# Top-64 attention: chunk tops stored rank by rank, selection behind its own chunks, ScalarE and TensorE in a new order, loops peeled

## Chip, cores and metric

One core of one Trainium2 chip (trn2) runs the whole program. The metric is the device time of one execution in microseconds; lower is better.

## The reference

The input is x, 2 images of 256 channels and 48x48 = 2304 positions. Two transformer-like layers follow each other. The first has top-k attention:

```python
q, k, v = heads(conv1x1(x, Wq, bq)), heads(conv1x1(x, Wk, bk)), heads(conv1x1(x, Wv, bv))
scores = einsum('bhnd,bhmd->bhnm', q, k) * 32 ** -0.5      # 8 heads of 32, N = 2304
kth = top_k(scores, 64)[0][..., -1:]
masked = where(scores >= kth, scores, finfo.min)
o = einsum('bhnm,bhmd->bhnd', softmax(masked), v)
o = conv1x1(o, Wo, bo) + x
h1 = relu(batchnorm(conv1x1(o, W1, b1)))
x = batchnorm(conv1x1(h1, W2, b2)) + o
```

The second normalises x over the channels, does full softmax attention of the same size, projects it and adds x. Everything is float32. The change touches only the first attention.

## The kernel before

The program is a sequence of stages, each a block in which every engine runs its own list of instructions and waits on semaphores: `project_heads`, `attention_top`, `project_out`, `mlp`, `project_heads`, `attention_full`, `output`. `attention_top` works on tiles of 128 queries against all 2304 keys. Two tiles make a pair; a head has 18 pairs (2 images x 9), and 8 heads make 144 pairs. What happens to a tile:

- TensorE computes the 128x2304 scores into `ps_s` (`score`, L363), ScalarE copies them to `scores_all` (`keep_scores`, L446), which has room for four tiles.
- VectorE takes the eight largest of each of 64 chunks of 36 scores (`chunk_tops`, MAX8, L557, into `top8`). `prepare` takes the eight largest of all that ranks 4 to 8 hold (L565, L567) and the largest of the ranks 1 and 8 (`extremes`, L568).
- ScalarE guesses a threshold from the chunk tops: a scaled sum of ranks 1 and 2 (`guess_place`, L477), then a count of candidates over it by Sign (L480, `balance`).
- VectorE's `select` corrects the guess (L582, L585), counts the candidates above it (L589), masks them (L594), computes `place` (L596), takes the best 24 of the rest in three rounds of MAX8 and MATCH_REPLACE8 (L601, L605), picks the one that is the 64th largest (L609) and flags rows where this can't be sure (`doubt`, L613).
- TensorE counts the flags (`count_doubts`, L390, L392), ScalarE copies the counts (`keep_any`, L467), and VectorE loads them into a register and branches (`hand_on`): where there is a doubt it counts the whole row again (L631) and, if need be, finds the threshold by eight full rounds (L644). Then it writes `steep_kth` (L666) and `minus_max` (L667).
- ScalarE writes a steep Relu penalty (L462), GpSimd subtracts it from the scores (L539), ScalarE takes the exponential with its sum (L450).
- TensorE transposes the 18 blocks of the tile in groups of four (`turn`, L373, two PSUM buffers `ps_t`), ScalarE copies each group (`keep_turned`, L457), TensorE weighs the values (`weigh`, L382). At the end of a pair ScalarE copies `parts` (L522), TensorE adds the quadrants (L401), ScalarE writes `o_all` (`finish`, L486).

The order within an engine is written out by hand. VectorE is a pair or more ahead: while it takes the chunk tops of pair p it selects pair p-1 behind the eighth chunk and hands it on behind the twentieth. ScalarE, in the step of pair p, makes the second guess of pair p+1 behind a copy of scores and the first guess of pair p+2 at the end. ScalarE and TensorE run `Fori(0, HEADS)` with 18 unrolled steps, and VectorE peels the first two pairs and the last head and runs `Fori(0, HEADS - 1)`. Past the last pair, ScalarE and TensorE still do the scores, guesses and penalties that their loop bodies hold.

Of the kernel before, what the change touches and what calls it, by code (L numbers as in the profile page):

```python
# [47 lines left out]
ROUNDS = TOPK // 8  # L48

# [223 lines left out]
def attention_top(nc, cst, operands, q_parts, k_parts, v_all, o_all, sums):  # L273
# [5 lines left out]
    with ctx:  # L279
# [13 lines left out]
        weighted, compared = sb("weighted", [P, 2, CHUNKS, 2]), sb("compared", [P, 2, CHUNKS, KEEP])  # L293
        minus_first, balance = sb("minus_first", [P, 2]), sb("balance", [P, 2])
        factor, guess = sb("factor", [P, 2]), sb("guess", [P, 2])
        above_guess, place = sb("above_guess", [P, 2]), sb("place", [P, 2])
        places, picked = sb("places", [P, WINDOW]), sb("picked", [P, 2, WINDOW])
        extremes, beyond = sb("extremes", [P, 2, 2]), sb("beyond", [P, 2])
# [22 lines left out]
        HEAD_PAIRS = B * PAIRS  # L321
        block = ctx.enter_context(nc.Block())
# [24 lines left out]
        def _(pe):  # L347
            pe.sem_inc(parts_ready, 1)
            pe.sem_inc(o_kept, 1)

            def score(s, h, tile, first=False):

                ahead, s = divmod(s, HEAD_TILES)
                b, pair = s // MCH, s // 2
                if s % 2 == 0:
                    pe.wait_ge(q_loaded[pair % AHEAD_Q],
                               (h + ahead) * (32 * HEAD_PAIRS // AHEAD_Q) + 32 * (pair // AHEAD_Q + 1))
                if s % MCH == 0:
                    pe.wait_ge(k_loaded[b], (h + ahead) * 64 + 64)
                if not first:  # L360
                    pe.wait_ge(scores_kept, tile)
                for c, n in SCOLS:
                    last = pe.matmul(ps_s[:, c:c + n], q_ring[pair % AHEAD_Q][:, P * (s % 2):P * (s % 2) + P],  # L363
                                     k_stack[b][:, c:c + n], start=True, stop=True)
                last.then_inc(scores_done, 1)

            def turn(s, g, tile):

                if s % 2 == 1 or g >= 2:
                    pe.wait_ge(turned_kept, tile * NTG + g - 1)  # L370
                m0, n = TGROUPS[g]
                for m in range(n):
                    last = pe.transpose(ps_t[(NTG * s + g) % 2][:, P * m:P * m + P],  # L373
                                        probs[s % 2][:, P * (m0 + m):P * (m0 + m) + P], cst["ident"][:, :])
                last.then_inc(turned, 1)

            def weigh(s, g, tile):
# [1071 lines left out]
```

## Time and profile before

| | |
|---|---|
| median of 3 runs | 5313.2 us (5310.25 to 5314.53) |
| profiled execution | 5306.61 us, span 5304.8 us |
| mean granted clock of TensorE | 0.825 |
| PE busy | 4161.1 us, 78% |
| DVE (VectorE) busy | 4384.5 us, 83% |
| ACT (ScalarE) busy | 4144.0 us, 78% |
| POOL (GpSimd) busy | 1502.1 us, 28% |

In the profile L-numbers are lines of the kernel. "Idle before" is the time an engine stood idle just ahead of an instruction or group, and behind the arrow stands what ended it; "issue" is a wait that the profile doesn't explain by a semaphore. On VectorE and ScalarE the next instruction may start a little before the last one has ended, so the distance of two starts is what an instruction costs its engine, and its duration is what someone who waits for its result sees.

### The profile page before, as it was taken

What the parts mean: (1) busy time and instruction counts of PE and PEld (TensorE: products, weight loads), DVE (VectorE), ACT (ScalarE), POOL (GpSimd) and SP (SyncE); (2) the same over time, 40 slices, a digit from 0 to 9 for tenths busy, and PEclk for the clock granted to TensorE, in tenths of its full rate; (3) what the DMA queues carried; (4) which work ended last, traced back from release to release, by engine and by line L of the source; (5) the groups of instructions that cost most, each with busy time, mean ns of one, the idle gap of its engine ahead of it and who ended that gap; (6) DMA issues with size and microseconds to landing.
All of it is one profiled execution on the core that took longest, in us unless ns stands there. A gap on an engine that the chain in (4) does not pass through costs nothing. (4 is left out here: it accounts for less than half of the span.)

```text
span 5304.8 us, 112543 instructions
## 1 busy us (share of the span) xinstructions
PE 4161.1 (78%) x32161; PEld 2808.6 (53%) x32161; DVE 4384.5 (83%) x25258; ACT 4144.0 (78%) x6082; POOL 1502.1 (28%) x362
## 2 busy tenths in 40 slices
PE   8576477776777557767777667798999999999997
PEld 4344345444444334444454445443567777777774
DVE  4899999998999899999999999430378888888885
ACT  2798599988998678988999889544268888888884
POOL 0354354444454334444454445100100000000000
PEclk9677677777777777777777777899799999999999
DMA  5000000000000000000000000100320101111012
GB/s 208 6 17 16 5 16 8 18 16 7 18 17 16 7 15 8 17 16 8 17 17 9 17 16 8 56 8 6 143 77 25 34 24 33 33 25 34 24 33 89
DMA packets 79566, 154.52 MB, mean 29 GB/s; under 512 B 8120, under 2 KB 49464, under 8 KB 73528
## 3 DMA queue, kind: packets, MB, share of 16 engines
q1 hardware_dynamic: 78904, 146.72, 9.8%
q8 instruction: 290, 4.75, 0.4%
q14 instruction: 372, 3.05, 0.2%
HBM read 99.50 MB, written 47.19 MB: 28 GB/s over the span
## 5 line engine op out<-in xcount | busy, mean ns | idle before, releaser
L539 POOL TENSOR_TENSOR a_probs<-a_scores,a_probs 128x2304 f32<-128x2304 f32 x288 | 1460.1, 5092 | 1778.5 <-ACT a_probs L462 1778.5
L557 DVE MAX8 a_top<-a_scores 128x8 f32<-128x36 f32 x18432 | 1830.8, 179 | 46.8 <-ACT a_scores L446 46.1
L373 PE MATMUL a_ps_t<-ident,a_probs 128*128 128x128 f32 x5184 | 973.7, 325 | 704.0 <-ACT a_probs_t L457 570.1
L373 PEld LDWEIGHTS a_ps_t<-ident,a_probs 128*128 128x128 f32 x5184 | 672.6, 164 | 992.2 <-ACT a_probs_t L457 708.6
L462 ACT ACTIVATE a_probs<-a_scores,a_steep_kth 128x2304 f32<-128x2304 f32 x290 | 641.2, 2211 | 295.0 <-DVE a_minus_max L667 295.0
L1117 PE MATMUL b_ps_t<-ident,b_soft 128*128 128x128 f32 x5184 | 744.1, 279 | 20.9 <-issue 19.3
L1242 DVE TENSOR_SCALAR_CACHE_REDUCE b_soft<-b_ps_s 128x2304 f32<-128x2304 f32 x288 | 735.2, 2553 | 26.9 <-PE b_ps_s L1101 9.0
L457 ACT ACTIVATE a_probs_t<-a_ps_t 128x512 f32<-128x512 f32 (+1 forms) x1440 | 727.2, 545 | 20.4 <-PE a_ps_t L373 7.4
L1117 PEld LDWEIGHTS b_ps_t<-ident,b_soft 128*128 128x128 f32 x5184 | 581.0, 141 | 204.0 <-issue 80.4
L1199 ACT ACTIVATE b_soft<-b_soft,b_minus_max 128x2304 f32<-128x2304 f32 x288 | 638.1, 2216 | 43.6 <-issue 26.0
L450 ACT ACTIVATE a_probs<-a_probs,a_minus_max 128x2304 f32<-128x2304 f32 x288 | 638.0, 2215 | 28.6 <-issue 18.5
L363 PE MATMUL a_ps_s<-a_k_stack,a_q_ring 128*128 128x512 f32 (+1 forms) x1465 | 647.5, 601 | 14.7 <-ACT a_scores L446 9.8
L446 ACT ACTIVATE a_scores<-a_ps_s 128x2304 f32<-128x2304 f32 x292 | 607.0, 2079 | 12.3 <-PE a_ps_s L363 12.3
L382 PE MATMUL a_ps_o<-a_probs_t,a_v 128*32 128x128 f32 x10368 | 579.0, 303 | 0.2
L1206 ACT ACTIVATE b_soft_t<-b_ps_t 128x512 f32<-128x512 f32 (+1 forms) x864 | 419.4, 520 | 174.6 <-PE b_ps_t L1117 174.3
L363 PEld LDWEIGHTS a_ps_s<-a_k_stack,a_q_ring 128*128 128x128 f32 x1465 | 433.2, 319 | 156.6 <-ACT a_scores L446 64.5
L1101 PE MATMUL b_ps_s<-b_k_stack,b_q_ring 128*128 128x512 f32 (+1 forms) x1440 | 451.0, 411 | 8.4 <-DVE b_soft L1242 5.0
L1248 DVE COPY b_soft_t<-b_ps_t 128x512 f32<-128x512 f32 x576 | 385.1, 687 | 83.1 <-PE b_ps_t L1117 82.7
L382 PEld LDWEIGHTS a_ps_o<-a_probs_t,a_v 128*32 128x32 f32 x10368 | 263.0, 115 | 226.0 <-issue 113.7
L1078 POOL COPY b_v<-v_all 128x576 f32 x16 | 10.6, 667 | 1293.1 <-PE b_ps_o L1136 1185.8
L1136 PE MATMUL b_ps_o<-b_soft_t,b_v 128*32 128x256 f32 x5184 | 368.5, 384 | 0.6 <-issue 0.6
L401 PE MATMUL a_ps_o<-add_up,a_parts 128*128 128x32 f32 x576 | 148.6, 397 | 259.1 <-ACT a_parts L522 259.1
(128 smaller groups left out, 4216.7 us busy)
## 6 DMA issues: line engine op xcount, KB each, us to landing
a_k_stack<-k_parts SPq DMA_DIRECT2D x72, 288.0 KB, 6.0
b_k_stack<-k_parts SPq DMA_DIRECT2D x72, 288.0 KB, 6.1
a_q_ring<-q_parts SPq DMA_DIRECT2D x294, 64.0 KB
b_q_ring<-q_parts SPq DMA_DIRECT2D x294, 64.0 KB
k_parts<-p_high SPq DMA_DIRECT2D x36, 256.0 KB, 2.1
k_parts<-p_rest SPq DMA_DIRECT2D x36, 256.0 KB, 2.2
q_parts<-p_high SPq DMA_DIRECT2D x36, 256.0 KB, 2.0
q_parts<-p_rest SPq DMA_DIRECT2D x36, 256.0 KB, 2.0
```

What stands on the lines that cost most here:

```text
L363: last = pe.matmul(ps_s[:, c:c + n], q_ring[pair % AHEAD_Q][:, P * (s % 2):P * (s % 2) + P], k_stack[b][:, c:c + n], start=True, stop=True)
L373: last = pe.transpose(ps_t[(NTG * s + g) % 2][:, P * m:P * m + P], probs[s % 2][:, P * (m0 + m):P * (m0 + m) + P], cst["ident"][:, :])
L382: last = pe.matmul(ps_o[rows, P * (s % 2):P * (s % 2) + P], v_s[s // MCH][:, m, :], probs_t[:, m, :], start=m < 4, stop=m + 4 >= MCH)
L446: act.activation(scores_all[:, s % 4, :], ps_s[:, 0:N], ACT.Copy).then_inc(scores_kept, 1)
L450: act.activation(probs[s % 2][:, :], probs[s % 2][:, :], ACT.Exp, scale=SCALE, bias=minus_max[parity][:, s % 2:s % 2 + 1], accum_out=sums[ ...
L457: act.activation(probs_t[:, m0:m0 + n, :], ps_t[(NTG * s + g) % 2][:, 0:n * P].rearrange("p (m q) -> p m q", q=P), ACT.Copy).then_inc(turn ...
L462: act.activation(probs[u][:, :], scores_all[:, 2 * parity + u, :], ACT.Relu, scale=-STEEP, bias=steep_kth[parity][:, u:u + 1]).then_inc(pe ...
L539: pool.tensor_tensor(probs[u][:, :], scores_all[:, 2 * (p % 2) + u, :], probs[u][:, :], ALU.subtract).then_inc(masked_ready, 1)
L557: last = dve.max(top8[s // 2 % 2][:, s % 2, c, :], scores_all[:, s % 4, CHUNK * c:CHUNK * c + CHUNK])
L1117: last = pe.transpose(ps_t[(NTG * s + g) % 2][:, P * m:P * m + P], soft[s % 3][:, P * (m0 + m):P * (m0 + m) + P], cst["ident"][:, :])
L1199: act.activation(soft[s % 3][:, :], soft[s % 3][:, :], ACT.Exp, scale=-1.0, bias=minus_max[s % 3][:, 0:1], accum_out=sums[:, s, cols(h + a ...
L1242: dve.tensor_scalar(soft[s % 3][:, :], ps_s[:, 0:N], -SCALE, None, ALU.mult, ALU.min, accum_out=minus_max[s % 3][:, 0:1]).then_inc(shifted ...
```

## The change

- `top8` is laid out rank by rank: eight places for the rest, then 64 values of rank 1, 64 of rank 2, and so on. MAX8 of a chunk writes its eight results 64 elements apart. The candidates are then one run of 8 + 3x64 = 200 elements (216 before, 16 of them fill). `extremes` come from MAX8 over 64 elements, two for each tile, in place of one reduction. `place` is gone, since `counts` holds 63 - n.
- VectorE selects a pair directly behind its own chunks, between `sort_rest` and the next pair, and hands it on behind the eighth chunk of the next pair. The wait for ScalarE's `balance` now stands behind the pair's own chunks.
- ScalarE makes both guesses of pair p+1 in the step of pair p: the first behind the exponential, the second behind two copies of transposes. The copies of scores move behind the first tile's last transpose copy and in between the second tile's last two; `finish` moves into the next step.
- TensorE has both score tiles of pair p+2 in the step of pair p, one behind the first tile's last `turn`, one behind the second tile's fourth.
- ScalarE and TensorE start two steps early with the parts that exist, loop over seven heads from pair 2 on, and peel the last; what would lie past the last pair is left out.

```diff
-        top8 = [sb(f"top8{n}", [P, 2, CHUNKS + REST, 8]) for n in range(2)]
-        below = sb("below", [P, 2, (CHUNKS + REST) * KEEP])
+        top8 = [sb(f"top8{n}", [P, 2, REST + 8 * CHUNKS]) for n in range(2)]
+        below = sb("below", [P, 2, CANDIDATES])
...
-                    last = dve.max(top8[s // 2 % 2][:, s % 2, c, :], scores_all[:, s % 4, CHUNK * c:CHUNK * c + CHUNK])
+                    last = dve.max(top8[s // 2 % 2][:, s % 2, REST + c:REST + c + 7 * CHUNKS + 1:CHUNKS], scores_all[:, s % 4, CHUNK * c:CHUNK * c + CHUNK])
...
+            rank = lambda tops, u, r, n=1: tops[:, u, REST + r * CHUNKS:REST + (r + n) * CHUNKS]
+            def sort_rest(pair, tops):
+                for u in range(2):
+                    wait_alone(dve, tops_taken, 2 * pair + u + 1)
+                    counted(dve.max(tops[:, u, 0:REST], rank(tops, u, KEEP, 7 - KEEP)))
+            def find_extremes(u, tops):
+                for n, r in enumerate((0, 7)):
+                    counted(dve.max(extremes[:, u, n, :], rank(tops, u, r)))
+            def correct_guess(pair):
                 after(at["n"])
                 dve.wait_ge(balance_ready, 2 * pair + 2)
-                factors = counted(dve.tensor_scalar(factor[:, :], balance[:, :], -STEP / 2,
-                                                    -(1.0 + STEP * (CHUNKS * KEEP / 2 - AIM)), ALU.mult, ALU.add))
+                return counted(dve.tensor_scalar(factor[:, :], balance[:, :], -STEP / 2,
+                                                 -(1.0 + STEP * (CHUNKS * KEEP / 2 - AIM)), ALU.mult, ALU.add))
...
-                counted(dve.tensor_scalar(place[:, :], above_guess[:, :], -1.0, TOPK - 1.0, ALU.mult, ALU.add))
...
             def pair_step(pair, tile, p, before=True):
+                tops = top8[p % 2]
                 def between(c):
                     if c == 7 and before:
-                        select(pair - 1, top8[(p - 1) % 2])
-                    if c == 19 and before:
                         hand_on(pair - 1, (p - 1) % 2)
                 chunk_tops(tile, 2 * p, between)
                 chunk_tops(tile + 1, 2 * p + 1)
-                prepare(pair, top8[p % 2])
+                sort_rest(pair, tops)
+                find_extremes(0, tops)
+                factors = correct_guess(pair)
+                find_extremes(1, tops)
+                select(tops, guess_of(factors))
```

ScalarE's step, before and after (`here`, `before`, `after` and `second` say whether the pair p, p-1, p+1 or p+2 exists; these tests are left out here):

```diff
-                    exponentials(s, h, tile, parity)
-                    keep_scores(s + 4, tile + 4)
-                    guess_place(1, pair + 1, 1 - parity)
-                    keep_turned(s, 0, tile)
-                    keep_turned(s, 1, tile)
-                    exponentials(s + 1, h, tile + 1, parity)
-                    keep_turned(s, 2, tile)
-                    keep_turned(s, 3, tile)
-                    keep_turned(s, 4, tile)
-                    keep_scores(s + 5, tile + 5)
-                    keep_any(pair + 1)
-                    keep_turned(s + 1, 0, tile + 1)
-                    keep_turned(s + 1, 1, tile + 1)
-                    act.wait_ge(kth_ready, pair + 2)
-                    penalty(0, 1 - parity)
-                    keep_turned(s + 1, 2, tile + 1)
-                    keep_turned(s + 1, 3, tile + 1)
-                    keep_turned(s + 1, 4, tile + 1)
-                    penalty(1, 1 - parity)
-                    act.wait_ge(weighed, tile + MCH + 3)
-                    act.activation(parts[:, :], ps_o[:, 0:PAIR], ACT.Copy).then_inc(parts_ready, 1)
-                    guess_place(0, pair + 2, parity)
-                    finish(s, h, pair)
+                exponentials(p, 0, h)
+                guess_place(p + 1, 0, h)
+                keep_turned(p, 0, 0, h)
+                finish(p - 1, h)
+                keep_turned(p, 0, 1, h)
+                guess_place(p + 1, 1, h)
+                keep_turned(p, 0, 2, h)
+                exponentials(p, 1, h)
+                keep_turned(p, 0, 3, h)
+                keep_turned(p, 0, 4, h)
+                keep_scores(p + 2, 0, h)
+                keep_turned(p, 1, 0, h)
+                keep_any(pair + 1)
+                keep_turned(p, 1, 1, h)
+                keep_turned(p, 1, 2, h)
+                penalty(p + 1, 0, h)
+                keep_turned(p, 1, 3, h)
+                keep_scores(p + 2, 1, h)
+                keep_turned(p, 1, 4, h)
+                penalty(p + 1, 1, h)
+                keep_parts(pair)
...
-            with act.Fori(0, HEADS) as h:
-                for p in range(HEAD_PAIRS):
+            for p in range(-2, 2):
+                pair_step(p, 0)
+            with act.Fori(0, HEADS - 1) as h:
+                for p in range(2, HEAD_PAIRS + 2):
+                    pair_step(p, h)
+            for p in range(2, HEAD_PAIRS):
+                pair_step(p, HEADS - 1)
+            finish(HEAD_PAIRS - 1, HEADS - 1)
```

TensorE's step after the change, in the same short form:

```
turn(p,0) groups 0 1 2 | weigh(p,0) 0 | turn 3 | weigh 1 | turn 4 | score(p+2,0)
turn(p,1) group 0 | weigh(p,0) 2 3 4 | turn(p,1) 1 | count_doubts(p+1) | turn(p,1) 2 3
score(p+2,1) | wait any_ready | weigh(p,1) 0 | turn(p,1) 4 | weigh(p,1) 1 2 3 4 | add_quadrants(p)
```

## Rows read from the trace of the kernel before

**Rows 1.** Page, costliest groups: count, busy us, mean ns, idle before

```profile
L450 ACT ACTIVATE a_probs<-a_probs,a_minus_max 128x2304 f32<-128x2304 f32 x288 | 638.0, 2215 | 28.6 <-issue 18.5
```

**Rows 2.** Timeline of VectorE over one ordinary pair: start us, duration us, instruction

```profile
944.99 0.88 DVE L557 MAX8 a_top<-a_scores 128x8 f32<-128x36 f32 x8 [0.18 <-ACT a_scores L446]
945.83 0.17 DVE L582 TENSOR_SCALAR a_factor<-a_balance 128x2 f32<-128x2 f32 x1
...
947.79 0.17 DVE L596 TENSOR_SCALAR a_place<-a_above_guess 128x2 f32<-128x2 f32 x1
...
951.42 0.16 DVE L613 SCALAR_TENSOR_TENSOR a_doubt<-a_beyond,a_kth 128x2 f32<-128x2 f32 x1
...
953.29 0.17 DVE L666 TENSOR_SCALAR a_steep_kth<-a_kth 128x2 f32<-128x2 f32 x1 [0.53 <-issue]
...
953.43 10.58 DVE L557 MAX8 a_top<-a_scores 128x8 f32<-128x36 f32 x108
963.93 0.48 DVE L565 MAX8 a_top<-a_top 128x8 f32<-128x320 f32 x1
...
964.72 0.61 DVE L568 TENSOR_REDUCE a_extremes<-a_top 128x4 f32<-128x256 f32 x1
965.50 0.88 DVE L557 MAX8 a_top<-a_scores 128x8 f32<-128x36 f32 x8 [0.17 <-ACT a_scores L446]
```

**Rows 3.** Timeline of ScalarE over the same pair

```profile
952.15 0.14 ACT L467 ACTIVATE a_any_doubt<-a_ps_o 1x3 f32<-1x3 f32 x1
...
953.56 2.22 ACT L462 ACTIVATE a_probs<-a_scores,a_steep_kth 128x2304 f32<-128x2304 f32 x1 [0.29 <-DVE a_minus_max L667]
...
960.36 0.23 ACT L486 ACTIVATE o_top<-a_ps_o 128x64 f32 x1
961.07 2.21 ACT L450 ACTIVATE a_probs<-a_probs,a_minus_max 128x2304 f32<-128x2304 f32 x1 [0.48 <-POOL a_probs L539]
...
963.28 2.07 ACT L446 ACTIVATE a_scores<-a_ps_s 128x2304 f32<-128x2304 f32 x1
965.25 0.30 ACT L477 ACTIVATE a_weighted<-a_top 128x128 f32<-128x128 f32 x1
...
966.04 0.19 ACT L480 ACTIVATION_READ_ACCUMULATOR a_compared<-a_top,a_minus_first 128x1 f32 x1
966.14 1.06 ACT L457 ACTIVATE a_probs_t<-a_ps_t 128x512 f32<-128x512 f32 x2
```

**Rows 4.** Timeline of GpSimd over the same pair

```profile
955.85 10.14 POOL L539 TENSOR_TENSOR a_probs<-a_scores,a_probs 128x2304 f32<-128x2304 f32 x2 [10.36 <-ACT a_probs L462]
```

**Rows 5.** Timeline of TensorE over the same pair

```profile
951.69 0.24 PE L392 MATMUL a_ps_o<-a_doubt,ones 128*1 128x1 f32 x4
951.86 0.65 PE L373 MATMUL a_ps_t<-ident,a_probs 128*128 128x128 f32 x4
...
963.43 1.97 PE L373 MATMUL a_ps_t<-ident,a_probs 128*128 128x128 f32 x8 [1.66 <-ACT a_probs L450]
```

**Rows 6.** The same timeline, cut after the first four transposes

```profile
963.43 1.12 PE L373 MATMUL a_ps_t<-ident,a_probs 128*128 128x128 f32 x4 [1.66 <-ACT a_probs L450]
```

**Rows 7.** Busy time in stretches: length, busy us, then PEclk 0.50, DMA

```profile
961.10:963.50 2.40, 0.74 (x4) 0.23 (x3) 2.40 (x26) 2.40 (x3) 2.40 (x1) 0.50 0.00 0
```

**Rows 8.** Groups of VectorE by form, 300 to 3300 us

```profile
L589 DVE TENSOR_SCALAR_CACHE_REDUCE a_below<-a_top,a_guess 128x216 f32<-128x216 f32 x267 | 106.3, 436 | 4.8
...
L631 DVE TENSOR_SCALAR_CACHE_REDUCE a_scratch<-a_scores,a_bound 128x2304 f32 x16 | 41.8, 2612 | 3.4 <-issue 3.4
```

**Rows 9.** Timeline of VectorE at a turn of the head loops

```profile
988.32 0.88 DVE L557 MAX8 a_top<-a_scores 128x8 f32<-128x36 f32 x8 [2.51 <-ACT a_scores L446]
```

**Rows 10.** Timeline at the start and the end of the stage

```profile
139.29 0.17 DVE L666 TENSOR_SCALAR a_steep_kth<-a_kth 128x2 f32<-128x2 f32 x1 [1.02 <-issue]
...
3348.28 0.17 DVE L666 TENSOR_SCALAR a_steep_kth<-a_kth 128x2 f32<-128x2 f32 x1 [1.70 <-ACT a_any_doubt L467]
...
3378.15 1.95 DVE L779 RECIPROCAL r_one_by_sum<-sums_top 128x288 f32<-128x288 f32 x1 [29.63 <-PEq L279]
```

More of the change, by code:

```diff
@@ L321, in attention_top, with exists @@
         HEAD_PAIRS = B * PAIRS
+        def exists(pair):
+            return not isinstance(pair, int) or 0 <= pair < ALL_PAIRS
         block = ctx.enter_context(nc.Block())
@@ L403, in add_quadrants, with pair_step @@
                 last.then_inc(added, 1)
-            score(0, 0, 0, first=True)
-            for s in range(1, 5):
-                score(s, 0, s)
-            count_doubts(0)
-            with pe.Fori(0, HEADS) as h:
-                for p in range(HEAD_PAIRS):
-                    pair, tile = h * HEAD_PAIRS + p, h * HEAD_TILES + 2 * p
-                    s = 2 * p
-                    pe.wait_ge(probs_ready, tile + 1)
-                    turn(s, 0, tile)
-                    turn(s, 1, tile)
-                    score(s + 5, h, tile + 5)
+            def pair_step(p, h):
+                pair = h * HEAD_PAIRS + p
+                here, after, second = exists(pair), exists(pair + 1), exists(pair + 2)
+                if here:
+                    for g in range(3):
+                        turn(p, 0, g, h)
@@ L429, in _ @@
-                    weigh(s, 4, tile)
-                    count_doubts(pair + 1)
-                    turn(s + 1, 1, tile + 1)
-                    turn(s + 1, 2, tile + 1)
-                    weigh(s + 1, 0, tile + 1)
-                    turn(s + 1, 3, tile + 1)
-                    weigh(s + 1, 1, tile + 1)
-                    turn(s + 1, 4, tile + 1)
-                    for g in range(2, NTG):
-                        weigh(s + 1, g, tile + 1)
-                    add_quadrants(pair)
-                    score(s + 6, h, tile + 6)
+                    if exists(pair - 1):
+                        pe.wait_ge(o_kept, pair)
@@ new lines, in pair_step @@
+                    weigh(p, 0, 0, h)
+                    turn(p, 0, 3, h)
+                    weigh(p, 0, 1, h)
+                    turn(p, 0, 4, h)
+                if second:
+                    score(p + 2, 0, h)
+                if here:
+                    turn(p, 1, 0, h)
+                    for g in range(2, NTG):
+                        weigh(p, 0, g, h)
+                    turn(p, 1, 1, h)
+                if after:
+                    count_doubts(pair + 1)
+                if here:
+                    turn(p, 1, 2, h)
+                    turn(p, 1, 3, h)
@@ new lines, in pair_step @@
+                if second:
+                    score(p + 2, 1, h)
+                if after:
+                    pe.wait_ge(any_ready, pair + 2)
+                if here:
+                    weigh(p, 1, 0, h)
+                    turn(p, 1, 4, h)
+                    for g in range(1, NTG):
+                        weigh(p, 1, g, h)
+                    pe.wait_ge(parts_ready, pair + 1)
+                    add_quadrants(pair)
+            for p in range(-2, 2):
+                pair_step(p, 0)
@@ L526, in _ @@
+            for p in range(-2, 2):
+                pair_step(p, 0)
+            with act.Fori(0, HEADS - 1) as h:
+                for p in range(2, HEAD_PAIRS + 2):
+                    pair_step(p, h)
+            for p in range(2, HEAD_PAIRS):
+                pair_step(p, HEADS - 1)
+            finish(HEAD_PAIRS - 1, HEADS - 1)
         @block.gpsimd
```

178 lines of the change are left out of this document (86 added, 92 removed).

## The prediction

> **What bounds the kernel now.** I read the page first for where the time lies. The stage that the change touches is the first attention, top-k included; it runs from about 113 to 3378 us [rows 10], some 62% of the span, and everything else is left alone. In it VectorE and ScalarE are both above nine tenths busy, so the shares don't say which of them sets the time. The timelines of one ordinary pair do: the eight chunk maxima that open a pair start at 944.99, the next ones at 965.50 [rows 2]. That is 20.51 us a pair, and it is one closed chain through all four engines:
>
> - eight chunks, then the guess's factor: 944.99 to 945.83, 0.84 [rows 2]
> - factor, guess and the whole selection to `doubt`: 945.83 to 951.42, 5.59 [rows 2]
> - doubt to `steep_kth`: 951.42 to 953.29, 1.87, of which ScalarE's copy of the doubt count starts 0.73 after the doubt, and the load, test and branch that follow take 1.14 [rows 2, 3]
> - to ScalarE's penalty 0.27, to GpSimd's subtraction 2.29 (955.85), from there to the exponential 5.22 (961.07) [rows 2 to 4]
> - exponential to the copy of the scores 2.21, that copy 2.07, and 0.15 until VectorE starts [rows 2, 3].
>
> The sum is 20.51. Every link is tight: VectorE's only idle time outside the branch ends with ScalarE's copy of the scores (0.17 at 965.50) [rows 2]. VectorE's own work is a second bound close below. From the first threshold at 139.29 to the last at 3348.28 there are 143 pairs in 3209 us [rows 10]: 143 x 20.5 = 2932, and the rest is recounts of doubtful rows (16 in the window of [rows 8], some with further rounds), a slower branch now and then, and seven turns of the head loop at some 2.6 us each ("issue" 18.5 us) [rows 1]. The change touches neither how often rows are doubtful nor what a recount costs.
>
> **VectorE's own work.** 120 of 128 chunk maxima are as before: 108 took 10.50 from 953.43 to 963.93, 0.097 apart [rows 2]; I expect no change from writing the eight results 64 elements apart. The selection reads 200 candidates in place of 216. A count over 216 elements lasts 0.436, the same instruction over 2304 2.612 [rows 8]: 1.04 ns an element, so 14 instructions (two counts, two masks, six maxima, four replacements) x 16 elements x 1.04 ns = 0.23 saved. `place` goes: 0.07 (947.79, next at about 947.86). The stretch from the first count to the doubt was 5.59 less 0.40 for factor and guess = 5.19, and becomes 4.88. The extremes' reduction starts at 964.72 and lasts 0.61 [rows 2], which keeps VectorE about 0.50; four maxima over 64 elements take its place, each, between 0.097 for 36 and 0.395 for 320 (963.93 to 964.72, two of them), 0.13, so 0.51: no gain. The factor now waits for the result of the maximum before it (0.24 in place of 0.13), and two maxima fill the gap between factor and guess, so from factor to first count 0.07 + 0.25 + 0.20 = 0.53. The whole: 0.14 + 120 x 0.097 + 0.79 + 0.37 + 0.53 + 4.88 + 0.60 + 1.14 = 20.1 us. Were VectorE the bound, that would be 0.4 less a pair.
>
> **Where the guess now stands.** Before, ScalarE's second guess stood behind the very copy of scores that VectorE's chunks waited for, and ended (966.23) while VectorE took eight chunks. Now VectorE selects a pair right behind its own chunks and must wait for ScalarE's second guess of that pair, which stands in ScalarE's queue behind the exponential of the pair before, the first guess, two copies of transposes and the finish. The closed chain is then, from the exponential's start:
>
> - Exponential: TensorE's transposes start 2.36 later (961.07 to 963.43) [rows 3, 5]. Four of them take 1.12 and eight 1.97 [rows 5, 6], and the first copy can't start before 3.51, the second before 4.36. ScalarE has come to 3.10 with exponential 2.21 and guess 0.89 (965.25 to 966.14), so it waits 0.41; a copy's 0.48 (an estimate, from two in 1.06) and finish 0.25 (0.23 at 960.36) bring it to 4.24, where it waits again 0.12. The second copy ends its turn at 4.84. VectorE's chunks for the second guess are done at 12.0 after `steep_kth` (0.14 + 56 and 64 chunks + 0.2); the guess starts at 0.27 + 7.51 + 4.84 = 12.6, so ScalarE, not VectorE, is late.
> - Guess to its count (966.04 + 0.19) 0.98 [rows 3], VectorE's start 0.12 as before (966.23 to 965.50 + 0.84).
> - Factor to doubt 0.53 + 4.88 = 5.41.
> - Doubt to the copy of the count: 0.73 before, where ScalarE was in a long copy; at least 0.54, since TensorE's counts end 0.51 after the doubt's start (951.69 + 0.24) [rows 5]. I take 0.60. Then 1.14 to `steep_kth`.
> - Penalty, subtraction, exponential: 0.27 + 7.51.
>
> Sum: 4.84 + 0.98 + 0.12 + 5.41 + 0.60 + 1.14 + 7.78 = 20.87, against 20.51: 0.36 longer. Over 143 pairs 51 us. The eight chunks in place of twelve before the branch are no matter: they end 0.9 after the doubt, while the branch ends at 1.74. ScalarE's own work is 20.51 less its idle 0.29 and 0.48 [rows 3], 19.7 us a pair, so it is no bound by busy time, and keeping the scores' copy off the path gains nothing more, since the path that went through it (20.51 less selection's saving) is replaced by this one.
>
> The bounds of that period: the copy of the count may start at 0.54 or, when TensorE is still in a transpose at the low clock ahead of `count_doubts`, at 0.8; the third copy of the odd tile stands between it and the penalty and may push it 0.2. So 20.8 to 21.1, 41 to 84 us.
>
> **Loops, start and end.** A turn of ScalarE's loop left it idle 2.6 us, and VectorE's turn fell inside VectorE's wait for that (2.51 at 988.32) [rows 1, 9]. There are now six turns of all three loops. VectorE's now lies between `doubt` and the branch, on the chain, uncovered. Priced as ScalarE's: 2.6 each, 0 if it hides after all, 3 at most. Six of ScalarE's, 0.2 of each hidden by the earlier end of its step, and six of VectorE's: 14 + 16 = 30 in place of 18, so +12 (-4 to +14).
> Start: the first threshold, at 139.29 [rows 10], came behind eight chunks of the next pair and a second guess; now the selection follows its own chunks at once, is 0.3 shorter, and the branch comes sooner. By the same working 1.1, 0.3 and 0.6, so -2. End: from the last `steep_kth` (3348.28) to the next stage's first VectorE instruction (3378.15) 29.9 us [rows 10], with a pair's scores, guesses and penalties that nobody uses. Without these the last step's chain is 7.8 to the exponential, then 14.3 through both tiles' copies to the finish, 0.5 to leave: 22.6, so -7.
>
> Sum: 51 + 12 - 2 - 7 = +54. The profiled execution took 5306.6 us, 1.8 of it beside its span, and the change would make it 5360.6; the median of the runs is 6.6 higher: **5367 us**.
>
> **Strides and turns against the Trainium skill.** A reading of ranks 3 of 8 apart costs no more per element here than one in a row: the count over 216 strided candidates takes 0.436 and the same instruction over 2304 in a row 2.612, 1.04 ns an element between them [rows 8].
> By the Trainium skill (SBUF — State Buffer, "Door 1: The DMA port swizzle", on SBUF's cachelines) accesses that go on to a new 16-byte line each time pay a penalty, which would favour the new layout's reads and speak against its spread writes. What it would do here stands as the fourth case below.
> Of the loops' turns, the Trainium skill (Runtime: NRT & Kernel Launch, "Instruction fetch mechanics") says that a taken branch to a page not at hand stalls for its fetch; the 2.6 us agree.
>
> **The cases.**
> 1. The forecast, 0.64: the guess's place sets 20.8 to 21.1 a pair; 5345 to 5400.
> 2. TensorE at the higher of its two levels when the transposes start, 0.12: for it, ScalarE would have the copies ready sooner (four transposes took 0.65 at 951.86) [rows 5]. Then ScalarE never waits, the guess starts at 2.21 + 0.89 + 0.48 + 0.25 + 0.48 = 4.31, the period is 20.34, and the sum -24 + 3 = -21: 5292, faster. It decides from 20.49 on, so when the second guess starts under 4.46 after the exponential. Against it: the granted clock is 0.50 there, 1.2 GHz [rows 7], although TensorE had a block of scores just ahead; the new order takes that away and leaves it idle through penalty and exponential.
> 3. The waits fall between, 0.11: a chain of 20.5 by a mixed clock or a shorter branch, the change lost in itself: 5303 to 5323.
> 4. Reads in a row are cheaper after all, 0.06: if the counts and masks owe 0.06 to strides (0.436 against the 0.37 that the 0.48 of the maximum over 320 gives for 216 elements), four of them on the chain save 0.24: 20.63, +20, 5333. Rows 8 speak against it.
> 5. The chunk maxima grow dearer by their spread writes, 0.07. At 6 ns each VectorE's own time rises by 0.8 to 20.9, which the forecast holds; at 10 ns more it passes it, 21.4, and the kernel is at 5440.
>
> Case 3 may end 0.02 on the faster side. So faster by over 0.2% 0.14, within 0.2% 0.09, slower 0.77 (10.6 us is about what a measurement can tell from no change). The range 5300 to 5400 leaves out case 2 and the far part of 5; the likeliest alone is 5345 to 5400.
>
> **What would show it.** On VectorE, idle time before the factor that ends with ScalarE's second guess, 0.75 us a pair or 110 in all, and none before the chunks; on ScalarE 0.4 us before the first copy behind each exponential, ended by TensorE; transposes there four in 1.12. Chunk maxima still 0.097 apart; six gaps of about 2.6 between a doubt and the next chunks. I am wrong if the exponential is followed by the second guess in under 4.4, if VectorE shows no wait ahead of the factor, or if the maxima have another duration.

## The result

The changed kernel takes 5840.08 us (median of 5 runs, 5839.0 to 5844.33); the kernel before, run beside it, 5314.3 us (5310.25 to 5315.77). The ratio is 1.0993 with a 95% interval of [1.0978, 1.1008]: 526 us slower, where the prediction had 54 and a range that ended at 5400. The direction came true, but not by what was forecast; the size did not.

From the page of the changed kernel, its span and engines:

```profile
span 5836.9 us, 112815 instructions
## 1 busy us (share of the span) xinstructions
PE 3978.4 (68%) x32130; PEld 2706.3 (46%) x32130; DVE 4782.5 (82%) x25830; ACT 4142.9 (71%) x6063; POOL 1497.9 (26%) x362
```

VectorE is busy 398 us longer, ScalarE and GpSimd as long as before: VectorE has more to do, not only more to wait for. Its groups by form name the work; first the kernel before, then the changed one (count, busy us, mean ns, idle before):

```profile
L631 DVE TENSOR_SCALAR_CACHE_REDUCE a_scratch<-a_scores,a_bound 128x2304 f32 x19 | 49.6, 2612 | 4.0 <-issue 4.0
...
L644 DVE MAX8 a_eight<-a_scratch 128x8 f32<-128x2304 f32 x16 | 41.0, 2560 | 1.2
L646 DVE MATCH_REPLACE8 a_scratch<-a_eight,a_scratch 128x2304 f32<-128x2304 f32 x16 | 40.7, 2543 | 0.0
```

```profile
L694 DVE MAX8 a_eight<-a_scratch 128x8 f32<-128x2304 f32 x104 | 266.3, 2561 | 7.6
L696 DVE MATCH_REPLACE8 a_scratch<-a_eight,a_scratch 128x2304 f32<-128x2304 f32 x104 | 264.5, 2543 | 0.0
...
L611 DVE MAX8 a_top<-a_top 128x8 f32<-128x256 f32 x288 | 106.4, 412 | 0.0
...
L681 DVE TENSOR_SCALAR_CACHE_REDUCE a_scratch<-a_scores,a_bound 128x2304 f32 x19 | 49.6, 2613 | 4.0 <-issue 4.0
```

L694 and L696 are `rounds_again`, the eight rounds over a whole row of scores that a tile goes through when its recount (L681) finds the threshold wrong. There are 19 recounts on both sides, counted by tile (L631 before, L681 now; [rows 8] has the 16 of its window). But 13 tiles go on to the eight rounds instead of 2 (104 and 16 instructions, eight a bout). They lie in 11 pairs: two pairs have two of them. The row between them tells why: the rest maximum reads 256 elements, not 320 as in [rows 2]. `rank(tops, u, KEEP, 7 - KEEP)` is four ranks, 4 to 7; before, `KEEP:8` was five, 4 to 8. A row is in doubt when the eighth value of some chunk, or the eighth of the rest, reaches the threshold. In the first case that value belongs among the candidates, and now it isn't there: the threshold is wrong and only the rounds mend it. The six recounts that still pass without rounds may be of the second kind; no run separates the two.

One such pair in VectorE's timeline (start us, duration us, instruction; the eight rounds are cut to the first and last):

```profile
1290.50 0.17 DVE L716 TENSOR_SCALAR a_steep_kth<-a_kth 128x2 f32<-128x2 f32 x1 [0.59 <-issue]
...
1314.22 2.61 DVE L681 TENSOR_SCALAR_CACHE_REDUCE a_scratch<-a_scores,a_bound 128x2304 f32 x1 [0.21 <-issue]
...
1320.74 2.56 DVE L694 MAX8 a_eight<-a_scratch 128x8 f32<-128x2304 f32 x1
...
1360.75 2.54 DVE L696 MATCH_REPLACE8 a_scratch<-a_eight,a_scratch 128x2304 f32<-128x2304 f32 x1
...
1363.80 0.17 DVE L716 TENSOR_SCALAR a_steep_kth<-a_kth 128x2 f32<-128x2 f32 x1 [0.28 <-issue]
```

From threshold to threshold 73.3 us, where a pair with a recount alone takes 28.8. Everything else waits meanwhile: GpSimd's idle time ahead of its subtractions, which ends with ScalarE's penalties, is 2315.7 us in all (1778.5 before).

An ordinary pair behaves as the prediction had it. "Ordinary" stands here and below for the shortest and most frequent kind: of the 143 distances from threshold to threshold 61 are 20.7 to 20.9 us and 54 are 21.0 to 21.2 (before: 20.4 to 20.7 and 20.75 to 21.1); what parts the two kinds comes in the last section. VectorE's timeline, answering [rows 2]:

```profile
951.75 0.17 DVE L716 TENSOR_SCALAR a_steep_kth<-a_kth 128x2 f32<-128x2 f32 x1 [0.81 <-issue]
951.83 0.16 DVE L717 TENSOR_SCALAR a_minus_max<-a_extremes 128x2 f32<-128x2 f32 x1
951.90 11.75 DVE L597 MAX8 a_top<-a_scores 128x8 f32<-128x36 f32 x120
963.55 0.74 DVE L611 MAX8 a_top<-a_top 128x8 f32<-128x256 f32 x2
...
965.46 0.17 DVE L622 TENSOR_SCALAR a_factor<-a_balance 128x2 f32<-128x2 f32 x1 [0.91 <-ACT a_compared L500]
...
970.86 0.16 DVE L663 SCALAR_TENSOR_TENSOR a_doubt<-a_beyond,a_kth 128x2 f32<-128x2 f32 x1
971.07 0.88 DVE L597 MAX8 a_top<-a_scores 128x8 f32<-128x36 f32 x8
972.56 0.17 DVE L716 TENSOR_SCALAR a_steep_kth<-a_kth 128x2 f32<-128x2 f32 x1 [0.61 <-issue]
```

A pair is 20.81 (951.75 to 972.56), and the idle time has moved to the factor and ends with ScalarE's second guess. ScalarE, answering [rows 3], shows what makes that guess late:

```profile
959.51 2.22 ACT L467 ACTIVATE a_probs<-a_probs,a_minus_max 128x2304 f32<-128x2304 f32 x1 [0.16 <-POOL a_probs L579]
...
963.03 0.60 ACT L474 ACTIVATE a_probs_t<-a_ps_t 128x512 f32<-128x512 f32 x1 [0.33 <-PE a_ps_t L379]
963.52 0.22 ACT L511 ACTIVATE o_top<-a_ps_o 128x64 f32 x1
963.88 0.60 ACT L474 ACTIVATE a_probs_t<-a_ps_t 128x512 f32<-128x512 f32 x1
964.38 0.30 ACT L497 ACTIVATE a_weighted<-a_top 128x128 f32<-128x128 f32 x1
```

Exponential 959.51, second guess 964.38: 4.87 later.

### The profile page after: what moved, and what is told of

Same layout as the page of the kernel before. It is cut to its first block and busy times, and to the rows that moved or that the text cites. A ratio compares the mean times of both kernels' runs of the same rounds, so it can differ in the third digit from the quotient of the medians.

```text
span 5836.9 us, 112815 instructions
## 1 busy us (share of the span) xinstructions
PE 3978.4 (68%) x32130; PEld 2706.3 (46%) x32130; DVE 4782.5 (82%) x25830; ACT 4142.9 (71%) x6063; POOL 1497.9 (26%) x362
## 5 line engine op out<-in xcount | busy, mean ns | idle before, releaser
L579 POOL TENSOR_TENSOR a_probs<-a_scores,a_probs 128x2304 f32<-128x2304 f32 x288 | 1456.0, 5076 | 2315.7 <-ACT a_probs L481 2315.7
L379 PE MATMUL a_ps_t<-ident,a_probs 128*128 128x128 f32 x5184 | 1072.9, 349 | 302.6 <-ACT a_probs L467 221.2
L379 PEld LDWEIGHTS a_ps_t<-ident,a_probs 128*128 128x128 f32 x5184 | 725.1, 175 | 584.5 <-ACT a_probs L467 242.7
L474 ACT ACTIVATE a_probs_t<-a_ps_t 128x512 f32<-128x512 f32 (+1 forms) x1440 | 764.8, 548 | 78.2 <-PE a_ps_t L379 56.7
L1162 PE MATMUL b_ps_t<-ident,b_soft 128*128 128x128 f32 x5184 | 748.1, 280 | 20.5 <-issue 19.0
L366 PE MATMUL a_ps_s<-a_k_stack,a_q_ring 128*128 128x512 f32 (+1 forms) x1440 | 383.5, 397 | 7.8 <-ACT a_scores L462 4.5
L366 PEld LDWEIGHTS a_ps_s<-a_k_stack,a_q_ring 128*128 128x128 f32 x1440 | 260.6, 198 | 50.1 <-issue 6.5
## 6 DMA issues: line engine op xcount, KB each, us to landing
a_k_stack<-k_parts SPq DMA_DIRECT2D x72, 288.0 KB, 6.0
b_k_stack<-k_parts SPq DMA_DIRECT2D x72, 288.0 KB, 6.0
```

Of the source, the lines that this page charges most:

```text
L366: last = pe.matmul(ps_s[:, c:c + n], q_ring[of_head % AHEAD_Q][:, P * u:P * u + P], k_stack[of_head // PAIRS][:, c:c + n], start=True, sto ...
L379: last = pe.transpose(ps_t[(NTG * u + g) % 2][:, P * m:P * m + P], probs[u][:, P * (m0 + m):P * (m0 + m) + P], cst["ident"][:, :])
L474: act.activation(probs_t[:, m0:m0 + n, :], ps_t[(NTG * u + g) % 2][:, 0:n * P].rearrange("p (m q) -> p m q", q=P), ACT.Copy).then_inc(turn ...
L579: pool.tensor_tensor(probs[u][:, :], scores_all[:, 2 * (p % 2) + u, :], probs[u][:, :], ALU.subtract).then_inc(masked_ready, 1)
```

## The experiments

Twelve kernels, each timed beside the kernel before, whose medians there were 5306 to 5309 us. There are 144 pairs. From the fifth kernel on the expectations multiply a pair's saving by 192, a slip; read with 143 they are a quarter smaller, and they are judged here by the pair's length too.

**e1_fifth_rank: the changed kernel with all five ranks in the rest.**

```diff
-                    counted(dve.max(tops[:, u, 0:REST], rank(tops, u, KEEP, 7 - KEEP)))
+                    counted(dve.max(tops[:, u, 0:REST], rank(tops, u, KEEP, 8 - KEEP)))
```

> The changed kernel, with the rest sorted over ranks 4 to 8 again (five ranks, 320 values) in place of ranks 4 to 7 (256). Theory A, the eighth rank's values are missing from the candidates, so a row whose chunk holds eight of the largest 64 gets a wrong threshold and goes through the eight full rounds: the full-row maxima (128x2304, MAX8) fall from 104 to 16, 11 bouts of 44.4 us less, 488 us, so 5352 us, 0.7% above the kernel before. Theory B, the loss lies in the new order's waits or the spread writes: the time stays above 5800 us.

Measured 5348.48 us, ratio 1.0078 [1.0064, 1.0091]. The rounds are back at 16 instructions:

```profile
L694 DVE MAX8 a_eight<-a_scratch 128x8 f32<-128x2304 f32 x16 | 41.0, 2560 | 1.2
```

From the first threshold to the last the changed kernel took 3743.07 us (137.94 to 3881.01), this one 3258.63 (140.60 to 3399.23): 484 less, 44.0 for each of 11 bouts. This is also the kernel that the prediction had priced: +42 us measured, +54 predicted, and inside the range of case 1.

**e2_before_four_ranks: the kernel before with four ranks, nothing else.**

```diff
-                counted(dve.max(tops[:, 0, CHUNKS:CHUNKS + REST, 0], tops[:, 0, 0:CHUNKS, KEEP:8]))
+                counted(dve.max(tops[:, 0, CHUNKS:CHUNKS + REST, 0], tops[:, 0, 0:CHUNKS, KEEP:7]))
```

(and the same for the second tile)

> The kernel before, with the rest sorted over ranks 4 to 7 only. Theory A: 104 full-row maxima in place of 16, 5314 + 488 = 5802 us, with the order of before unchanged. Theory B, the loss belongs to the new order: 5314 us, unchanged.

Measured 5794.18 us, ratio 1.0917 [1.09, 1.0934], again with 104 full-row maxima:

```profile
L644 DVE MAX8 a_eight<-a_scratch 128x8 f32<-128x2304 f32 x104 | 266.3, 2560 | 7.7
```

One rank less in the old kernel gives nine tenths of the loss (488 of 526 us), without any of the new order or layout.

**e3_guess_before_copy: e1 with the second guess ahead of the second copy of transposes.**

```diff
-                    keep_turned(p, 0, 1, h)
                 if after:
                     guess_place(p + 1, 1, h)
                 if here:
+                    keep_turned(p, 0, 1, h)
```

> The changed kernel with five ranks, and ScalarE's second guess one place earlier, ahead of the second copy of transposes. Theory A, a pair is the closed chain through ScalarE's second guess: the guess starts 4.27 in place of 4.86 us after the exponential, 0.55 us a pair less (VectorE's own work of about 20.2 is then as long as the chain), 78 us, so 5274 us, below the kernel before. Theory C, another wait takes its place (the transposes at the low clock, or the chunk maxima): 5352 us, as with five ranks alone.

Measured 5291.33 us, ratio 0.9975 [0.9964, 0.9986]: 57 us faster than e1 and faster than the kernel before. The guess's place was what set e1's pair. An ordinary pair is 20.33 us, and the gain stops there. VectorE and then ScalarE over one pair:

```profile
967.37 0.89 DVE L596 MAX8 a_top<-a_scores 128x8 f32<-128x36 f32 x8 [0.27 <-ACT a_scores L462]
968.73 0.17 DVE L715 TENSOR_SCALAR a_steep_kth<-a_kth 128x2 f32<-128x2 f32 x1 [0.48 <-issue]
```

```profile
960.33 0.31 ACT L497 ACTIVATE a_weighted<-a_top 128x128 f32<-128x128 f32 x1
...
965.12 2.10 ACT L462 ACTIVATE a_scores<-a_ps_s 128x2304 f32<-128x2304 f32 x1
967.09 0.62 ACT L474 ACTIVATE a_probs_t<-a_ps_t 128x512 f32<-128x512 f32 x1
967.56 0.14 ACT L486 ACTIVATE a_any_doubt<-a_ps_o 1x3 f32<-1x3 f32 x1
```

Another loop stands at 20.33. From `steep_kth` through the other 120 chunks to the next guess (at 960.33 + 20.33) it takes 11.93; from the guess back to `steep_kth` 8.40, by two paths at once. One goes through the scores: to the end of their copy 6.89 (967.22), 0.15 to VectorE's chunks, 0.88 for eight, 0.48 for the branch. The other goes through the count: 7.23 to its copy (967.56), then 1.17. My reading at the time was ScalarE's queue and the second path alone; e5, e10, e11 and e12 test it.

**e4_layout_alone: the kernel before, its order kept, with the rank-by-rank layout, 200 candidates and no `place`.**

```diff
-                    last = dve.max(top8[s // 2 % 2][:, s % 2, c, :], scores_all[:, s % 4, CHUNK * c:CHUNK * c + CHUNK])
+                    last = dve.max(top8[s // 2 % 2][:, s % 2, REST + c:REST + c + 7 * CHUNKS + 1:CHUNKS], scores_all[:, s % 4, CHUNK * c:CHUNK * c + CHUNK])
...
-                candidates = lambda u: tops[:, u, :, 0:KEEP]
+                candidates = lambda u: tops[:, u, 0:CANDIDATES]
```

> The kernel before in its own order and loops, with the rank-by-rank layout alone (200 candidates in one run, extremes by four short maxima, no place, five ranks in the rest). Theory A, the selection lies on the chain there too and is 0.31 us shorter: 143 x 0.31 = 44 us less, 5270 us. Theory D, spread writes make the chunk maxima dearer, or the saving is lost in the wait for the copy of the scores: 5314 us or more.

Measured 5308.89 us, ratio 1.0003 [0.9994, 1.0012]: no gain, a miss. The selection is 0.3 shorter, but ScalarE's copy of the count doesn't follow. ScalarE, then VectorE:

```profile
941.88 2.21 ACT L451 ACTIVATE a_probs<-a_probs,a_minus_max 128x2304 f32<-128x2304 f32 x1
...
951.49 2.09 ACT L447 ACTIVATE a_scores<-a_ps_s 128x2304 f32<-128x2304 f32 x1
953.46 0.14 ACT L468 ACTIVATE a_any_doubt<-a_ps_o 1x3 f32<-1x3 f32 x1
```

```profile
952.42 0.16 DVE L615 SCALAR_TENSOR_TENSOR a_doubt<-a_beyond,a_kth 128x2 f32<-128x2 f32 x1
...
954.90 0.17 DVE L668 TENSOR_SCALAR a_steep_kth<-a_kth 128x2 f32<-128x2 f32 x1 [1.14 <-issue]
```

The count copy stands behind a copy of scores and comes 1.04 after the doubt, 0.73 before ([rows 2, 3]). So the kernel before has a second path of the same length: exponential, ScalarE's own queue to the count copy, branch, penalty, exponential. In e4 it takes 11.58 from exponential to count copy, with no idle time on ScalarE between, then 1.12 to `steep_kth` in an ordinary pair and 7.78 to the next exponential, 20.48 in all; the kernel before has 11.59 for the first part (940.56 to 952.15). The prediction had called its chain the only one.

**e5_scores_copy_earlier: e3 with the first copy of scores and its matmuls ahead of the first tile's copies 3 and 4.**

```diff
                     exponentials(p, 1, h)
+                if second:
+                    keep_scores(p + 2, 0, h)
                     keep_turned(p, 0, 3, h)
                     keep_turned(p, 0, 4, h)
-                if second:
-                    keep_scores(p + 2, 0, h)
```

> The kernel with the second guess ahead of the copy, and besides the first copy of the scores (L462) and its matmuls moved ahead of the copies 3 and 4 of the first tile's transposes. There VectorE waits 0.27 us a pair for that copy (it ends 967.22, the doubt was there at 966.93). Theory A: the pair is set by ScalarE's own queue from the exponentials (956.17) to the count copy (967.56) with hardly an idle moment, and the same operations stand ahead of the count copy in either order, so only VectorE's wait changes its place, to before steep_kth: 5291 us within 10. Theory B: VectorE's wait for the scores is what sets the pair: 192 times 0.27 = 52 us less, 5240.

Measured 5544.6 us, ratio 1.0454 [1.044, 1.0468], far from both. TensorE and ScalarE:

```profile
1027.67 0.66 PE L379 MATMUL a_ps_t<-ident,a_probs 128*128 128x128 f32 x4 [2.19 <-ACT a_probs_t L474]
1028.26 0.85 PE L389 MATMUL a_ps_o<-a_probs_t,a_v 128*32 128x128 f32 x20
1029.04 0.66 PE L379 MATMUL a_ps_t<-ident,a_probs 128*128 128x128 f32 x4
1029.62 0.19 PE L397 MATMUL a_ps_o<-a_doubt,ones 128*1 128x2 f32 x2
```

```profile
1029.95 0.16 ACT L486 ACTIVATE a_any_doubt<-a_ps_o 1x3 f32<-1x3 f32 x1 [0.99 <-PE a_ps_o L399]
```

ScalarE's work ahead of the count copy is the same, but TensorE's transposes and products wait for the late copies, and the count of doubts stands behind them in TensorE's queue: 2 us too late. The run doesn't decide its question; it shows that a copy moved on one engine moves everything queued behind it on the engine that waits.

**e6_guess_first_old_layout: e3 with the tops in the old layout** (216 candidates, `place`, one reduction for the extremes; the reverse of e4's diff).

> The kernel with the second guess ahead of the copy, but with the chunk tops in before's layout (216 candidates, the place computed, the extremes by one reduction), so that the selection costs its 0.3 us a pair more again. Theory A: the selection is not what ends last there (ScalarE's queue up to the count copy is), so the doubt may come up to 0.3 later and most of it is slack: 5291 to 5310 us. Theory B: guess, selection, doubt and count are one chain that sets the pair, and the layout's 0.3 us stand on it: 192 times 0.3 = 58 us more, 5349.

Measured 5306.93 us, ratio 1.0003 [0.9994, 1.0012]: 16 us above e3, an ordinary pair 20.51 against 20.33. The layout's 0.3 us is worth 0.18 here: part of it is slack before the copy of the scores. With e4, the layout alone gives nothing, the order with the old layout nothing, both with the guess well placed 0.25%.

**e7_tensore_kept_busy: e1 with 24 more matmuls a pair in TensorE's idle stretches**; their product isn't used.

```diff
+            def keep_busy(n):
+                for _ in range(n):
+                    pe.matmul(ps_t[0][:, 0:P], cst["ident"][:, :], cst["ident"][:, :], start=True, stop=True)
...
-                    for g in range(1, NTG):
+                    for g in range(1, NTG - 1):
                         weigh(p, 1, g, h)
+                    keep_busy(8)
+                    weigh(p, 1, NTG - 1, h)
+                    keep_busy(9)
                     pe.wait_ge(parts_ready, pair + 1)
                     add_quadrants(pair)
+                    keep_busy(7)
```

> The changed kernel with the fifth rank, and 24 more matmuls of the identity by itself a pair on TensorE in its idle stretches behind the second tile's last copies and behind the parts (their product stands in columns of the transposes' tile that the next transposes overwrite; nobody reads it). Case 2 of the prediction: the granted clock is 1.0 instead of 0.5 when the first three groups of transposes run (2.92 us for 12 there), the copies no longer wait 0.33 to 0.48 us for them, the second guess comes 4.3 to 4.4 us after the exponentials' start instead of 4.86: some 0.45 us a pair, 86 us, down to where ScalarE's own queue stops it: 5262 to 5300 us. Rival: the copies' wait was slack, or the clock does not follow: 5348 within 10.

Measured 5299.64 us, ratio 0.9989 [0.998, 0.9998]: 49 us less than e1, at the upper end of the expectation for case 2. Ordinary pairs are 20.15 us, but the 14 that follow a recount take 21.1 to 22.8, 17 us more in all than in e1. TensorE behind a recount:

```profile
1129.35 0.65 PE L389 MATMUL a_ps_o<-a_probs_t,a_v 128*32 128x128 f32 x8 [8.74 <-ACT a_probs_t L483]
1129.93 3.78 PE L413 MATMUL a_ps_t<-ident 128*128 128x128 f32 x16
```

After 8.74 idle the eight extra matmuls (16 records) last 3.78 at a granted clock of 0.50, against 2.05 in an ordinary pair, and delay the product behind them.

**e8_guess_first_kept_busy: the same 24 in e3.**

> The same 24 more matmuls a pair in the kernel with the second guess ahead of the copy. There ScalarE waits 0.33 us a pair for the first transposes (idle before L474 at 959.68), and that is the only idle time in the stretch from the exponentials to the count copy. Theory A (ScalarE's queue from the exponentials to the count copy sets the pair): the count copy starts 0.3 earlier, the pair takes 20.1 instead of 20.33, where VectorE's own work of about 20.1 us stops it: some 44 us less, 5240 to 5255. Rival: 5291, since VectorE is the limit already.

Measured 5311.65 us, ratio 1.0012 [1.0003, 1.0021]: not faster but 20 us above e3. The ordinary pair stays at 20.33: the wait for the transposes is gone, and 0.34 appears where VectorE's chunks aren't ready yet.

```profile
965.99 0.31 ACT L506 ACTIVATE a_weighted<-a_top 128x128 f32<-128x128 f32 x1 [0.34 <-DVE a_top L605]
```

That is e3's loop seen from the other side: with the guess first, ScalarE waits for VectorE. In e7 the second copy of transposes fills that time. The 20 us lie in the 14 pairs that follow a recount: 307.7 us together, 288.0 in e3, the same price of the extra matmuls as in e7.

**e9_half_the_extra_matmuls: e1 with 4 + 4 + 4 of them.**

> The changed kernel with the fifth rank and 12 extra matmuls a pair (4 in each of the three idle stretches) instead of 24. With 24 the ordinary pair took 20.15 us instead of 20.81, but every pair behind a recount or a turn of a loop 1.5 to 2.4 us more, since 8 of them take 3.78 us at the lower clock (2.05 at the higher) and TensorE comes late. Theory: with 12 the extra work fits its idle 5.2 us a pair even at the lower clock; if the clock still holds, the ordinary pair stays near 20.15 and the pairs behind a recount go back: some 20 to 26 of them by 1.5 us, 5300 - 35 = 5265 us. Rival: 12 leave too much idle time, the clock falls back as without them, and the time goes back to 5348 within 10.

Measured 5282.08 us, ratio 0.996 [0.9947, 0.9974], the best of all: the ordinary pair 20.14, and 12 of the 14 pairs that follow a recount 20.1 to 20.5 again. Stretches of TensorE under the transposes, first the changed kernel, then e9 (length, then busy us, the clock in the third column from the end):

```profile
961.90:964.70 2.80, 2.80 (x12) 2.26 (x12) 2.65 (x23) 2.29 (x9) 2.80 (x2) 0.50 0.01 3
```

```profile
1063.90:1065.90 2.00, 1.71 (x16) 1.31 (x17) 2.00 (x20) 1.97 (x8) 2.00 (x1) 1.00 0.00 0
```

The clock is 1.2 GHz there and 2.4 GHz here, where the extra matmuls run in the idle stretches. The second guess comes 4.15 after the exponential (1061.57 to 1065.72), in time for VectorE. In 18 of the pairs it comes 4.8 to 4.9 after it, as in e1, and the pair is longer: the granted clock is 0.50 there (2786.7 to 2788.9 us in one of them), so twelve matmuls didn't keep the higher clock every time.

**e10_count_copy_earlier: e3 with `keep_any` ahead of `keep_turned(p, 1, 0)` on ScalarE.**

> The kernel with the second guess ahead of the copy, and besides the count copy (L486) ahead of the first copy of the second tile's transposes (967.09 to 967.56 there) on ScalarE. Theory A (ScalarE's queue from the guess to the count copy is part of what sets the pair): the doubt is there at 966.93 and its count on TensorE 0.2 to 0.3 us later, so the count copy starts at about 967.25 instead of 967.56, 0.3 a pair times 192 = 58 us less, 5233; stopped by VectorE's own 20.1 us it would be 5250. Theory B (VectorE's own work sets the pair already): no change, 5291 within 7.

Measured 5302.7 us, ratio 0.9991 [0.9982, 1.0], the ordinary pair still 20.33 to 20.34. The count copy did come earlier, 7.04 behind the guess instead of 7.23, and `steep_kth` did not:

```profile
1079.60 0.89 DVE L595 MAX8 a_top<-a_scores 128x8 f32<-128x36 f32 x8 [0.37 <-ACT a_scores L462]
1080.97 0.17 DVE L714 TENSOR_SCALAR a_steep_kth<-a_kth 128x2 f32<-128x2 f32 x1 [0.49 <-issue]
```

It stands 1.37 behind the start of the chunks, 1.36 in e3 (967.37 to 968.73): the path through the scores holds alone. Theory A is refuted, and theory B too, since VectorE still waits twice here. Neither had the time: the kernel is 11 us above e3. In 48 of its pairs the next guess comes 12.1 to 12.6 behind `steep_kth` instead of 11.93, in e3 in 8. Why ScalarE is later there was not tested.

**e11_both_ends_earlier and e12_reading_earlier_alone: the counts read behind 5 chunks instead of 8**, in e10 and in e3.

```diff
-                    if c == 7 and before:
+                    if c == 4 and before:
```

> The kernel with the second guess ahead of the copy and the count copy earlier, and besides the reading of the counts on VectorE behind 5 chunks of the next pair instead of 8. Theory: two paths end at steep_kth within 0.03 us of each other: the copy of the scores ends, then 8 chunks (0.84 us) and load and branch (0.49 us); and the count copy starts, then 1.14 to 1.17 us. The count copy alone earlier gained nothing because the first path stood. With both earlier steep_kth comes 0.2 us sooner (1079.61 + 1.14 = 1080.75 instead of 1080.97): 192 times 0.2 = 40 us below the kernel with the earlier count copy alone, 5263 us within 10. Rival: VectorE's own work sets the pair, no change: 5303 within 10.

> The kernel with the second guess ahead of the copy (5291 us), and the reading of the counts on VectorE behind 5 chunks of the next pair instead of 8, the count copy where it was. Theory: no change, 5291 within 8, since the count copy starts at 967.56 and 1.14 behind it is 968.70, where steep_kth stands already (968.73). Rival: the copy of the scores and the chunks behind it are the only bound, and three chunks less (0.29 us) are 192 times 0.29 = 56 us less: 5235.

Measured 5324.8 us (1.0028 [1.0017, 1.0039]) and 5330.76 us (1.0036 [1.0022, 1.005]): some 33 and 39 slower than e3, against every expectation. VectorE, then ScalarE, in e12:

```profile
1086.45 0.17 DVE L715 TENSOR_SCALAR a_steep_kth<-a_kth 128x2 f32<-128x2 f32 x1 [0.78 <-issue]
...
1105.79 0.59 DVE L596 MAX8 a_top<-a_scores 128x8 f32<-128x36 f32 x5 [0.46 <-ACT a_scores L462]
1107.15 0.17 DVE L715 TENSOR_SCALAR a_steep_kth<-a_kth 128x2 f32<-128x2 f32 x1 [0.77 <-issue]
```

```profile
1098.67 0.31 ACT L497 ACTIVATE a_weighted<-a_top 128x128 f32<-128x128 f32 x1 [0.22 <-DVE a_top L596]
...
1106.02 0.15 ACT L486 ACTIVATE a_any_doubt<-a_ps_o 1x3 f32<-1x3 f32 x1
```

The three chunks are not taken away, they move behind `steep_kth`, onto the part that both paths share: to the next guess 12.22 instead of 11.93, and ScalarE now waits for VectorE there. The count copy keeps its place behind the guess (7.23 in most pairs, as in e3; 7.35 in the one shown, which is 20.70) and `steep_kth` its place behind the copy (1.13 here, 1.15 in most). So an ordinary pair is 12.22 + 7.23 + 1.15 = 20.60, 0.27 more, times 143 the 39 us. It also shows the path through the count holding alone, with the one through the scores three chunks shorter. In e11 both paths are shorter, 8.31 from guess to `steep_kth` instead of 8.40, and the pair is 20.55. What the expectations left out is that chunks ahead of the branch lie under its wait, and cost nothing there.

## Why the prediction was wrong, and where it held

- **The step that failed** is "The change touches neither how often rows are doubtful nor what a recount costs". The first half is true, 19 recounts on both sides; the second is false. What a doubtful tile costs depends on whether the recount finds the threshold wrong, and that depends on which ranks the candidates hold. The term was set to nothing and measured 484 us (11 bouts of 44.0), shown alone in both directions by e1 and e2.
- **Where it could have been read.** The sum of VectorE's own work carries 0.79 for the two rest maxima, taken from the rows over 320 elements, though the diff's `7 - KEEP` makes them 256. Checking that shape against the diff would have shown the missing rank, and the kernel's 2 bouts among 19 recounts would have priced it: up to 17 more. No case of the five held it. The last condition named ("or if the maxima have another duration") came true in the rest maxima, 412 ns where e1 has 476 for 320 elements, but it was written of the chunk maxima, which kept theirs.
- **The new chain held.** With the fifth rank back the ordinary pair is 20.81 (predicted 20.87): exponential to second guess 4.87 (4.84), factor to doubt 5.40 (5.41), count copy to `steep_kth` 1.13 to 1.2 in 67 pairs (1.14), but 1.36 to 1.53 in 53. The wait before the factor is 137.0 us in the changed kernel and 118.0 in e1 (predicted 110), the one before the first copy 0.33 (0.41). The 101 pairs of e1 without a recount or a turn, and not just behind a recount, average 20.95 us, 106 such pairs of the kernel before 20.67: 0.27 longer, where 0.36 was forecast. Times 143 that is 39 of the 50 us that lie between first and last threshold (51 of 63 in the sum), so the pair's length is the term that makes +54 out of +42.
- **Turns** in e1 cost ScalarE 2.8 to 3.0 as read from the pairs (23.6 to 23.9), and VectorE 1.4 to 1.9 (22.2 to 22.7), where 2.6 each was taken. VectorE stands idle 2.9 to 3.2 at its turn, more than the 2.6; the rest lies under the wait for the count. **Start**: the first threshold by itself tells nothing, since the moment at which the first scores are there moves by 2.7 us between two profiles of kernels that start alike (first threshold 137.94 in the changed kernel, 140.60 in e1). From VectorE's first chunk to the first threshold it is 21.4 us in both, 23.15 before, so 1.7 earlier (predicted 2). **End**: 3881.01 to 3904.15 is 23.1 us (predicted 22.6).
- **A reading that was off**: ScalarE isn't above nine tenths busy in the stage. From 113 to 3378 us VectorE has 92%, ScalarE 87%. No term was taken from it.
- **The loop of before** was right as a sum, but "one closed chain" was wrong: e4 shows an equal path through ScalarE's queue, so a shorter selection would have given nothing there.
- **Case 2** (the higher clock) didn't happen by itself, 0.50 again under the transposes; made to happen in e9 it gives 5282, 24 below the kernel before where 21 was priced. That is partly luck: the ordinary pair is 20.14, not 20.34, and 18 pairs stay at the lower clock.
- **Case 4** (reads in a row cheaper) is refuted by the 5.40 and by the count itself: 436 ns over 216 strided candidates, 419 over 200 in a row, 1.06 ns for each of the 16, which length alone gives. **Case 5** (spread writes dearer) as well: 120 chunk maxima still take 11.65 to the next start, 0.097 each. The Trainium skill (SBUF — State Buffer, "Door 1: The DMA port swizzle") has a penalty for accesses that change the 16-byte line each time; MAX8 with results 64 elements apart shows none (0.097 from start to start before and after).

## What to carry to other kernels

When a diff rewrites an index range in a stage whose slow path depends on data, count the elements on both sides before timing anything: the trace gives the price of the slow path (here 44 us a bout, 2 bouts among 19 recounts), and the result can stay the same while its cost goes up more than sixfold, to 13 bouts. Before giving a saving its worth, look for a second path of the same length; here two or three paths ended within 0.1 us of each other, and single edits gave nothing or a loss. Moving one copy also moves every product and count queued behind it on the engine that waits.

## What was not expected of the hardware

- A few matmuls whose product nobody reads, put into TensorE's idle stretches, paid for themselves: granted clock 1.00 instead of 0.50 under the transposes, pair 20.81 to 20.14, mean clock 0.94 against 0.84, kernel 66 us faster. Twice as many gave 18 us of it back: after a long idle time they ran at the lower clock themselves (8 in 3.78 us instead of 2.05), and the 14 pairs that follow a recount take 310 us together, 286 with half as many.
- The same load, test and branch on VectorE takes 1.11 to 1.2 us behind the count copy in some pairs of the unrolled step and 1.36 to 1.53 in others, by place in the code: in the kernel before, the pairs at places 4, 8, 11, 12, 15 and 16 of 18 (counted from 0) are the slower ones in each of heads 1 to 6, 20.8 where they are otherwise undisturbed, and most others 20.5. In e1 eight places of 18 are slower ones. What in the place makes the difference is not shown. The prediction had one value for all.
